# One mixture-of-experts block on one core: the head of the program put in another order

## What is computed

```python
xn = layernorm(x)
# attention: q, k, v, o weights are basis @ coeffs.T, 32 wide
scores = (xn @ q_w) @ (xn @ k_w).T * decay ** max(diff - 1, 0) * (diff > 0)
att = (scores @ (xn @ v_w)) @ o_w.T * out_scale
# router: two largest of 4 logits, softmax over them
e0 = silu(xn @ sw_w1) * (xn @ sw_w3) @ sw_w2
e1 = gelu((((xn @ eq + b) @ wv + b) @ wo + b) @ c1 + b) @ c2 + b
e2 = (layernorm(h2 + relu(h2 @ f1 + b) @ f2 + b) * g + b) @ gen + b   # h2 = layernorm(syn + attn)
e3 = gelu(xn @ ml_w1 + b) @ ml_w2 + b
out = x + att + sum of the two chosen experts, weighted
```

## Time and profile before

| | us |
|---|---|
| runs | 443.36, 443.31, 444.12 |
| median | 443.36 |
| profiled execution, its own time | 443.12 |
| its span, first to last instruction | 440.9 |
| busy in the span: PE, DVE, ACT, POOL | 429.6, 386.5, 275.9, 328.3 |

### The profile page before, as it was taken

The page is one execution under the profiler, slowest core; times in us unless marked ns, Lnnn a source line. Parts: engine busy times, 40 slices in busy tenths (PEclk is TensorE's granted clock), DMA queues, the critical chain, the costliest instruction groups (busy, mean ns, idle before and its releaser), DMA issues.

```text
span 440.9 us, 9655 instructions
## 1 busy us (share of the span) xinstructions
PE 429.6 (97%) x2760; PEld 366.8 (83%) x2760; DVE 386.5 (88%) x1229; ACT 275.9 (63%) x534; POOL 328.3 (74%) x478
## 2 busy tenths in 40 slices
PE   4989999999999999999999999999999999999997
PEld 4868888888887888888888888888888888888876
DVE  5685998998989899898998999889899989998887
ACT  4883856658385674837568384665838567483851
POOL 3798497786859778695986859688685977868394
PEclk9999999999999999999999999999999999999999
DMA  7514315234251432424243251423325152341301
GB/s 263 41 45 105 69 46 123 49 92 78 73 106 37 116 74 79 87 71 95 48 106 80 75 96 63 104 48 96 70 71 111 32 134 56 89 79 49 73 1 48
DMA packets 120322, 35.03 MB, mean 79 GB/s; under 512 B 96912, under 2 KB 114032, under 8 KB 120304
## 3 DMA queue, kind: packets, MB, share of 16 engines
q1 hardware_dynamic: 120016, 34.80, 33.5%
q10 hardware_dynamic: 288, 0.01, 0.0%
HBM read 18.60 MB, written 15.99 MB: 78 GB/s over the span
## 4 chain that ended last, share of the span: by engine, by line
PE 96%; ACT 1%; DMA 1%; DVE 1%; issue 0%; SPq 0%; DVEq 0%
PE S L1183 15%; PE S L1185 13%; PE S L1184 13%; PE EX L1107 12%; PE EX L1127 6%; PE S L1284 3%; PE S L1289 3%; PE S L1285 3%; PE EX L1137 3%; PE S L1196 2%; PE S L1297 2%; PE S L1295 2%; PE S L1296 2%; PE S L1197 2%; PE S L1198 2%; PE ATT L1209 2%
## 5 line engine op out<-in xcount | busy, mean ns | idle before, releaser
L503 POOL TENSOR_TENSOR hid3l<-hid,hid3h 128x512 fp32r<-128x512 f32 x64 | 80.8, 1293 | 59.7 <-ACT hid3h L647 59.7
L1183 PE MATMUL S<-xh,WH 128*128 128x512 f32 x224 | 91.9, 410 | 0.0
L1185 PE MATMUL S<-xh,WL 128*128 128x512 f32 x224 | 88.3, 394 | 0.0
L1184 PE MATMUL S<-xl,WH 128*128 128x512 f32 x224 | 88.2, 394 | 0.0
L1107 PEld LDWEIGHTS EX<-scaled,hid 128*128 128x128 f32 x480 | 55.9, 192 | 1.3
L1107 PE MATMUL EX<-scaled,hid 128*128 128x128 f32 x480 | 56.0, 275 | 0.0
L803 DVE SCALAR_TENSOR_TENSOR OUT<-EX,coef,OUT 128x128 f32<-128x128 f32 x184 | 51.6, 344 | 1.0
L568 ACT CAST xh<-TR 128x512 fp32r<-128x512 f32 x16 | 9.4, 588 | 65.7 <-DVE TR L860 64.5
L1185 PEld LDWEIGHTS S<-xh,WL 128*128 128x128 f32 x224 | 42.1, 188 | 10.0
L1183 PEld LDWEIGHTS S<-xh,WH 128*128 128x128 f32 x224 | 42.1, 188 | 8.4
L621 ACT COPY kv<-S 128x192 f32<-128x192 f32 x64 | 20.5, 320 | 45.5 <-PE S L1198 44.7
(11 more groups left out here) (199 smaller groups left out, 1070.9 us busy)
## 6 DMA issues: line engine op xcount, KB each, us to landing
X<-x SPq DMA_DIRECT2D x16, 256.0 KB, 2.8
turning<-xn SPq DMA_DIRECT2D x15, 256.0 KB, 2.6
xb<-turning SPq DMA_DIRECT2D x60, 64.0 KB, 2.6
turning<-e3T SPq DMA_DIRECT2D x15, 256.0 KB, 2.1
turning<-u SPq DMA_DIRECT2D x15, 256.0 KB, 2.3
e3b<-turning SPq DMA_DIRECT2D x60, 64.0 KB, 2.7
ub<-turning SPq DMA_DIRECT2D x60, 64.0 KB, 2.7
out<-OUT SPq DMA_DIRECT2D x15, 256.0 KB, 2.3
```

Of the source, the lines that this page charges most:

```text
L503: pool.tensor_tensor(hid3l[:, j, :], hid[3][:, j, :], hid3h[:, j, :], ALU.subtract) \
L1183: pe.matmul(bank[:, :], wh, hi, start=True, stop=False)
L1184: pe.matmul(bank[:, :], wh, lo, start=False, stop=False)
L1185: pe.matmul(bank[:, :], wl, hi, start=False, stop=True).then_inc(unit_ready, 1)
```

## The change

It moves instructions and adds none but idle products. (1) `DECAY_BEFORE_X` goes from 8 to 2, so x's moments come before decay steps 3 to 10. (2) The normalisation of xn on VectorE moves ahead of the low parts `TL`. (3) TensorE's five 64-wide idle products are taken out, seven 128-wide ones (identity times identity) are put at the very start, as soon as GpSimd has made the identity, and five instead of three stand behind the transposes. (4) ScalarE casts piece 0 of the weights ahead of the `TH` casts; `back`'s copies, `backh`, `gen_s`, the broadcast and piece 2's cast move into group 0's turn. (5) `backl` on VectorE moves behind `times(1)`. (6) `fold_first` on TensorE moves from behind the token tiles to behind `f1`. (7) GpSimd normalises group 1's x before, no longer after, it makes the low part of weight piece 2.

```diff
-                    norm_x(g.next())            # GpSimd, now ahead of low_weights
...
             act.copy(TH[:, P:LOGW], w("router")).then_inc(setup_act, 1)
+            high_weights(0)
             act.wait_ge(setup_mm, MM.index("ce") + 1)
...
-            high_weights(0)
-            act.wait_ge(pool_const, POOL_CONSTS)
-            act.wait_ge(setup_act, 1)
-            for t in range(NT):
-                act.copy(back[t * C:(t + 1) * C, t * P:(t + 1) * P], oT[:, :]).then_inc(back_laid, 1)
             take_x(Group(0, 0))
-            act.wait_ge(back_laid, NT)
-            act.copy(backh[:, :], back[:, :]).then_inc(back_high, 1)
             high_weights(1)
...
                 if first:
-                    for n in range(FIRST_SPLITS, len(WEIGHT_SPLITS)):
-                        high_weights(n)
-                if first:
+                    lay_back()
                     act.wait_ge(depth_loaded, DMA_INC)
...
                 half_gate(0)
+                if first:
+                    high_back()
...
                 half_gate(1)
+                if first:
+                    scale_gen()
+                    for n in range(FIRST_SPLITS, len(WEIGHT_SPLITS)):
+                        high_weights(n)
...
+            pe.wait_ge(pool_const, IDENT_CONSTS)
+            for _ in range(IDLE_FIRST):
+                pe.matmul(ATT[:, 0, :], ident[:, :], ident[:, :], start=True, stop=True)
             pe.wait_ge(w_loaded[LOAD_OF["ce_x0"]], DMA_INC)
...
-            idle_products(IDLE_BEFORE, P // 2)
             turn_x(Group(0, 0))
...
-DECAY_BEFORE_X = 8
-IDLE_BEFORE = 5
-IDLE_BEHIND = 3
+DECAY_BEFORE_X = 2
+IDLE_FIRST = 7
+IDLE_BEHIND = 5
+IDENT_CONSTS = 6
```

More of the change, by code:

```diff
@@ L498, in turn @@
                 if first:
+                    norm_x(g.next())
                     low_weights(range(FIRST_SPLITS, len(WEIGHT_SPLITS)))
-                    norm_x(g.next())
                 for j in range(4):
@@ L592, in _, with lay_back, high_back, scale_gen @@
             act.copy(TH[:, 0:P], prod("ce")).then_inc(fold_high, 1)
-            high_weights(0)
-            act.wait_ge(pool_const, POOL_CONSTS)
-            act.wait_ge(setup_act, 1)
-            for t in range(NT):
-                act.copy(back[t * C:(t + 1) * C, t * P:(t + 1) * P], oT[:, :]).then_inc(back_laid, 1)
             take_x(Group(0, 0))
-            act.wait_ge(back_laid, NT)
-            act.copy(backh[:, :], back[:, :]).then_inc(back_high, 1)
             high_weights(1)
-            act.wait_ge(w_loaded[LOAD_OF["gen_w"]], DMA_INC)
-            act.mul(gen_s[:, :], w("gen_w"), vec("n2g")).then_inc(setup_act, 1)
-            act.copy(bcast[:, 1, :], vec("n2b").broadcast_to([P, P])).then_inc(setup_act, 1)
+            def lay_back():
+                act.wait_ge(pool_const, POOL_CONSTS)
+                act.wait_ge(setup_act, 1)
+                for t in range(NT):
+                    act.copy(back[t * C:(t + 1) * C, t * P:(t + 1) * P], oT[:, :]).then_inc(back_laid, 1)
+            def high_back():
+                act.wait_ge(back_laid, NT)
+                act.copy(backh[:, :], back[:, :]).then_inc(back_high, 1)
+            def scale_gen():
+                act.wait_ge(w_loaded[LOAD_OF["gen_w"]], DMA_INC)
+                act.mul(gen_s[:, :], w("gen_w"), vec("n2g")).then_inc(setup_act, 1)
+                act.copy(bcast[:, 1, :], vec("n2b").broadcast_to([P, P])).then_inc(setup_act, 1)
             def turn(g, first, last):
@@ L719, in _ @@
             assert step[0] == DECAY_STEPS
+            dve.wait_ge(first_root, 1)
+            for t in range(NT):
+                dve.tensor_scalar(xn[:, t, :], X[0][:, t, :], negmean["x"][:, t:t + 1], rstd["x"][:, t:t + 1],
+                                  ALU.add, ALU.mult).then_inc(x_normed, 1)
             taken = [0]
@@ L741, in _ @@
             took(dve.tensor_tensor(TL[:, 0:P], prod("ce"), TH[:, 0:P], ALU.subtract))
[L742 to L745, removed]
             dve.wait_ge(setup_act, 2)
@@ L756, in _ @@
             x_low(Group(0, 0))
-            dve.wait_ge(back_high, 1)
-            dve.tensor_tensor(backl[:, :], back[:, :], backh[:, :], ALU.subtract).then_inc(back_low, 1)
             dve.wait_ge(vec_loaded, DMA_INC)
@@ L945, in turn @@
                 if first:
+                    dve.wait_ge(back_high, 1)
+                    dve.tensor_tensor(backl[:, :], back[:, :], backh[:, :], ALU.subtract).then_inc(back_low, 1)
                     fold_first()
@@ L1200, in turn @@
                 if first:
-                    fold_first()
-                if first:
                     pe.wait_ge(split_low, 1)
@@ L1265, in turn @@
                 if first:
+                    fold_first()
                     attend()
```

## The result

The changed kernel is slower, by a third of a percent. Over 22 runs its median is 443.80 us (443.18 to 446.50), that of the kernel before, over 22 runs beside it, 442.35 (441.20 to 444.12). The ratio is 1.0033, 95% interval 1.0019 to 1.0046. I had forecast 441.7. The three runs of before that I had seen (443.3 to 444.1) were at the slow end of what it does.

A forecast was written before the change was run, and what follows sets the result against it. TensorE, busy 97%, was taken as the bound, its last hole ending at the product with `back`. 2.85 us gained at the first `kv` copy, less 1.2 on ScalarE, gives 1.65: 443.36 to 441.7 us, range 441.0 to 443.4.

The forecast's parts named there:

- The frame: TensorE's work behind the product with `back` is packed and unchanged; only that product's start, 28.06 before, counts.
- The steps up to `xh`: At the head, moments start 1.5 us earlier, `xn` at 8.47 not 9.86, transposes end at 10.1 to 10.7, `xh` follows.
- The low parts and the casts: Behind `xn` on VectorE, four `TL` subtractions and the `tokb` copy take 1.1 us, ending near 10.7; `TH` casts just in time.
- VectorE: Behind `times(1)`, `backl` (0.7) and the `me1`, `gen` copies (0.75) end about 25.75, hidden before `foundl` with 0.2 us to spare.
- The clock: TensorE's early idle products bring 2.4 GHz before the transposes; first `kv` copy at 12.2 against 15.03, 2.85 us earlier.
- rival B: TensorE's clock level rises only around 11 to 12 us, transposes 0.6 later; gain 1.0, time 442.35 us; chance 0.18.
- The base: Starting point: profiled execution of the kernel before, 443.12 us, median 443.36, product with `back` at 28.06.
- ScalarE's toll: Between `kv` copies and `foundh`, 2.22 us of added work less waits of 0.46 and 0.50: net cost 1.2 to 1.3.
- C: Rival: clock level rises at 15 again, idle records hold the tiles until 12.7; 0.6 us late, 443.9; chance 0.12.
- D: Rival: ScalarE's waits stay, or x lands 0.6 later and transposes slip; gain 0.63, time 442.7 us; chance 0.18.

The follow-up runs named there:

- e5: e1 plus `backl` made by GpSimd between its two normalisations instead of by VectorE; median 441.74 us, ratio 0.9993 to the kernel before.
- e3: Changed kernel with GpSimd's first low-weights operation cut into four of 256 columns; median 442.05 us, ratio 0.9999 to the kernel before.
- e4: Kernel before with the router's low-part subtraction moved behind the copy of `tokb`, 0.25 us later; one profiled execution, 445.41 us.
- e1: Changed kernel with VectorE making the router's low part ahead of the four `xn` tiles; median 442.76 us, ratio 0.9999 to the kernel before.
- e2: Changed kernel with fourteen instead of five idle products behind the transposes; median 443.59 us, ratio 1.0026 to the kernel before.
- e7: e5 plus eight idle products on TensorE ahead of its wait for `h2l`; median 441.48 us, ratio 0.9979 to the kernel before.
- e10: Changed kernel with fourteen idle products behind the transposes and e7's eight, both VectorE stalls left in; median 443.69 us, ratio 1.0036 to the kernel before.
- e6: Kernel before, unchanged, profiled a second time; this execution took 442.23 us.
- e11: Kernel before with part 3 of the change alone, the idle products; median 441.55 us, ratio 0.9987 to the kernel before.

## Why the prediction was wrong

**The frame was right.** All is decided at the product with `back`; from there to the end it is 412.7 to 413.2 us in every profile above but e5's, where the clock was still low behind it (414.5).

**The steps up to `xh` were right.** Moments 5.38 (forecast 5.1), `xn` 8.81 (8.47; the decay row itself began 0.2 later), last transpose 10.3, upper level by 7.5. And e3, with the first stall gone, has `foundh` where I had put it, at 25.68 for 25.65.

**The step that failed is "The low parts and the casts".** It put four subtractions and a copy at 1.1 us, "near 10.7". They ended at 12.6. My 1.1 counts 0.15 us for the router's part from a place where GpSimd was idle, and sets it at a place where GpSimd was at work; in the same text I had GpSimd start at 9.7. I checked slack against the casts and not against the neighbour. The Trainium skill (SBUF — State Buffer, "SBUF: two separate sides") says it outright: a VectorE instruction with two SBUF inputs and a GpSimd instruction that reads SBUF share one pair of ports, and whichever starts first keeps it for its whole instruction. The trace agrees, both ways: 2.34 us for a 128x4 operation in e4, and 1.72 instead of 1.30 for GpSimd's `hid3l` behind `backl`. It was the page to weigh, and the prediction named another.

**The same error again in "VectorE".** `backl` was put at 0.7, "as the other 128x512 difference `xl`". `xl` reads one input from PSUM, the memory into which TensorE's products go: `TR` lies there, and `xl` takes 0.69 in every trace here, with GpSimd at work beside it or not; `backl` reads both from SBUF. Same shape, not the same price: it measured 1.53, and 0.74 of that was late for `foundl`.

**"The clock" was half right.** It rose when forecast, in this execution; in e5's, with the same list on TensorE up to there, it rose near 11, which is rival B's condition. That it could fall again, once the stall had left TensorE idle for 2 us, was in no case. Nor was the hole ahead of `f1`, 1.2 us in the kernel before, 1.5 in the changed kernel's profile and 1.7 in e1, e2, e3 and e5; none of the listed runs of before, 79 of them beside the experiments, has a mean granted clock under 0.999. The profiled loss adds up: from e7's 26.45, 1.6 for the first stall (`xl` 12.61 and 10.99), 0.8 for the low level (`foundh` 28.14 against 27.33 in e10), 0.7 for the second stall make 29.6; measured 29.69.

**The base was unlucky and could have been doubted.** I worked from one execution in which the level rose at 15.0. Another of the same program has it 4.8 us sooner (e6). Of those 79 runs of before (without the far one), 52 have a span of 439.6 to 440.5 and 27 one of 440.9 to 441.8; my 440.9 belongs to the second kind. I had weighed that the moment may differ between executions only for a rival of the change, not for the kernel before. The fair base was 442.4 by time and 439.9 to 440.2 by span, and the 1.65 us that I forecast is what the idle products alone give from that execution: in e11 the product with `back` starts at 26.36, 1.7 before 28.06.

**ScalarE's toll was right in size.** Net 1.2 to 1.3 forecast; 12.03 to 13.23 measured, that is 1.2. Its meaning I missed: it cancels the reordering's own gain (1.1 us) to within 0.1, so without the clock the sum is about zero (e11 against e7; the two differ in more than the order, as said).

**The rivals.** C had the sign but not the cause: it held the level low until 15, and the level was high by 7.5. B's condition came true in e5's execution, not in this one. D's first form did not happen: ScalarE does not wait before Q or `foundh` in the changed kernel's profile. Its second, that the chain slips because "several slacks above are 0.2 us or less", had the shape but priced it at 1.1 us too little.

## What to carry to other kernels

When an instruction is moved, ask what each other engine does at its new time, above all GpSimd beside a VectorE instruction whose two inputs are both in SBUF: take its duration from a place with the same company, or count GpSimd's whole instruction. Put such small operations ahead of GpSimd's long ones, cut the long ones (e3), or let one input come from PSUM, as with `xl`, which was not tried as an edit. And before a gain is credited to order, look whether the clock in the profiled head is the typical one, and compare spans beside times. Eight idle products in a hole of 1.7 us are all that parts e5 (spans 439.5 to 442.8) from e7 (439.4 to 439.8). They are no guarantee: two of e10's twelve runs show a fall with both holes filled.

## What was not expected of the hardware

A start 0.03 us behind GpSimd's and not 0.16 ahead of it turned 0.15 into 2.34 us. The level of one program rose at 10.2 in one execution and at 15.0 in another, and with one instruction moved at 18.3. The granted clock fell to 1.2 GHz behind idle stretches of only 1.7 to 2.0 us, but not always: e3's profile has such a hole (PE busy 0.34 of 2.00 us between 21 and 23) and stayed at 1.00. What decides between the two was not found. When it fell, it stayed low for 3.4 us in one execution and almost 7 in another (e5).
